# VectorE instead of ScalarE scales the inner rows of a ternary network to integers

## What is computed

```python
def _quant_act(x):
    s = jnp.max(jnp.abs(x), axis=-1, keepdims=True) / 127.0 + EPS
    xq = jnp.clip(jnp.round(x / s), -128.0, 127.0)
    return (xq, s)

def _qlinear(x, w):
    wq, ws = _quant_weight(w)
    xq, xs = _quant_act(x)
    y = jnp.einsum('bsi,oi->bso', xq, wq)
    return y * xs * ws
...
gate = jax.nn.silu(_qlinear(x, w_gate))
up = _qlinear(x, w_up)
return _qlinear(gate * up, w_down)
```

## Time and profile before

| | |
|---|---|
| median of three runs | 478.23 us (477.91 to 479.02) |
| span of the profiled execution, first to last instruction | 476.0 us |
| TensorE busy | 399.1 us |
| VectorE busy | 375.6 us |
| ScalarE busy | 301.7 us |
| granted TensorE clock, mean over the span | 0.956 of full |

### The profile page before, as it was taken

One profiled execution on the slowest core, in us unless ns is written; L12 is line 12 of the kernel. 1 busy time (PEld: TensorE's weight loads), 2 busy tenths in 40 slices (PEclk: granted clock), 3 DMA queues, 4 the chain that ended last, 5 costly groups with the idle time before them and its releaser, 6 DMA issues.

```text
span 476.0 us, 7786 instructions
## 1 busy us (share of the span) xinstructions
PE 399.1 (84%) x2612; PEld 191.0 (40%) x2612; DVE 375.6 (79%) x801; ACT 301.7 (63%) x442; POOL 0.2 (0%) x4
## 2 busy tenths in 40 slices
PE   1041866677786999999999999999999999999996
PEld 1010344333334445544434333554444444444443
DVE  5999599999998989999986975895456677777754
ACT  5888686689795865678976677463234444444422
POOL 0000000000000000000000000000000000000000
PEclk9995699689898899999999999999999999999999
DMA  8520000000003360383433233244413556653101
GB/s 294 227 67 0 1 1 1 1 1 0 2 2 101 121 211 24 93 232 117 138 104 109 89 110 109 83 143 149 145 67 134 170 168 170 169 172 130 67 22 44
DMA packets 31506, 47.47 MB, mean 100 GB/s; under 512 B 5610, under 2 KB 15210, under 8 KB 30956
## 3 DMA queue, kind: packets, MB, share of 16 engines
q1 hardware_dynamic: 31468, 46.98, 31.6%
HBM read 45.65 MB, written 1.31 MB: 99 GB/s over the span
## 4 chain that ended last, share of the span: by engine, by line
PE 60%; DVE 21%; ACT 9%; issue 5%; DMA 2%; SPq 2%; DVEq 0%; ACTq 0%
PE ps L1622 32%; PE ps L1956 16%; PE ps L1731 4%; PE ps L1719 2%; DVE bn L1044 1%; ACT regO L608 1%; SPq L563 1%; DVE xn L1063 1%; PE ps L1741 1%; DMA regC<-in_ctxT_dram 1%; PE ps L1647 1%; ACT regW L629 1%; PE ps L1613 1%; DVE regO L1272 1%; DVE kc L1178 1%
## 5 line engine op out<-in xcount | busy, mean ns | idle before, releaser
L1529 DVE TENSOR_TENSOR regW<-ps,regW 128x512 f32<-128x512 f32 x64 | 44.1, 690 | 53.8 <-PE ps L1622 51.2
L1622 PE MATMUL ps<-hH,regC 128*128 128x512 f16 x264 | 85.5, 379 | 0.0
L959 ACT ACTIVATE regW<-ps 128x512 f32<-128x512 f32 x51 | 30.4, 596 | 85.0 <-PE ps L1622 82.0
L1622 PE MATMUL ps<-hH,regW 128*128 128x512 f16 x248 | 81.5, 384 | 1.1 <-DVE regW L1529 1.1
L1622 PE MATMUL ps<-hL,regC 128*128 128x512 f16 x132 | 50.0, 379 | 0.0
L1956 PE MATMUL ps<-regW,regC 128*128 128x512 f16 x198 | 48.2, 379 | 0.0
L1622 PE MATMUL ps<-hL,regW 128*128 128x512 f16 x124 | 47.5, 383 | 0.0
L1512 DVE TENSOR_TENSOR regW<-regW 128x512 f16<-128x512 f32 x64 | 43.6, 682 | 0.7 <-ACT regW L972 0.5
L1956 PE MATMUL ps<-regW 128*128 128x512 f16 x180 | 43.8, 379 | 0.2 <-DVE regW L1512 0.2
L972 ACT CAST regW<-regW 128x512 f16<-128x512 f32 x64 | 39.2, 613 | 2.0 <-DVE regW L1550 1.8
L1622 PEld LDWEIGHTS ps<-hH,regC 128*128 128x128 f16 x264 | 25.8, 98 | 31.6 <-issue 2.3
(11 more groups left out here) (210 smaller groups left out, 692.2 us busy)
## 6 DMA issues: line engine op xcount, KB each, us to landing
regW<-routing_dram SPq DMA_DIRECT2D x130, 128.0 KB, 3.0
fw<-in_gu_dram SPq DMA_DIRECT2D x31, 256.0 KB, 3.1
regP<-in_gu_dram SPq DMA_DIRECT2D x25, 256.0 KB, 3.1
fw<-in_dp_dram SPq DMA_DIRECT2D x31, 128.0 KB, 3.1
regP<-in_dp_dram SPq DMA_DIRECT2D x25, 128.0 KB, 3.1
regO<-in_ffn_dram SPq DMA_DIRECT2D x3, 1024.0 KB, 9.2
x<-in_x_dram SPq DMA_DIRECT2D x2, 512.0 KB, 8.2
regC<-in_ctxT_dram SPq DMA_DIRECT2D x1, 1024.0 KB, 5.2
```

Source lines behind the costliest of these rows:

```text
L959: nc.scalar.activation(sgm[:, c % 2, :], bank(gate_bank(c)), ACT.Silu, scale=UNSCALE).then_inc(esilu_done, 1)
L1529: V.tensor_tensor(rows, bank(gate_bank(c) + 1), rows, ALU.mult).then_inc(et_done, 1)
L1622: mm = T.matmul(out_ap, w(k), a(k), start=(n == 0), stop=(n == 3 * DK - 1))
```

## The change

VectorE scales each tile at the end of `hidden_scale`, in one instruction (multiply by `rhs`, add MAGIC) that waits for its own reciprocal and, from tile 1 on, for `hz_turned`. ScalarE's `ffn_scale` and its eight calls are gone. What is computed is the same, and no buffer changes.

```diff
@@ BESIDE_SCALAR
             (0, "A"): [("turned_weights", 0, 1), ("weights_high", 5), ("wide_silu", 5, 0, 6), ("weights_high", 6),
-                ("ffn_scale", 4), ("wide_silu", 5, 1, 4)],
+                ("wide_silu", 5, 1, 4)],
             (1, "A"): [("ffn_turned", 4, 6)],
-            (2, "A"): [("ffn_scale", 5), ("wide_silu", 6, 0, 4)],
+            (2, "A"): [("wide_silu", 6, 0, 4)],
...
-            (5, "A"): [("ffn_scale", 7), ("project", 5, 6)],
+            (5, "A"): [("project", 5, 6)],
@@ block.scalar
-            def ffn_scale(t):
-
-                act.wait_ge(hscale_ready, t + 1)
-                if t >= 1:
-                    act.wait_ge(hz_turned, t)
-                nc.scalar.activation(fz, fhp[:, t % 2, :], ACT.Identity, bias=magic[:, 0:1],
-                                     scale=rhs[:, t:t + 1]).then_inc(hz_ready, 1)
...
             ffn_silu(2, 2)
-            ffn_scale(0)
             ffn_silu(3, 4)
             table_exp_ln()
-            ffn_scale(1)
             ffn_turned(0, 4)
-            ffn_scale(2)
             ffn_turned(1, 0)
             ffn_turned(2, 6)
-            ffn_scale(3)
@@ block.vector
                 post(V.tensor_tensor(so[:, t:t + 1], tiny[:, 1:2], wdt[:, :], ALU.mult))
+                dve.wait_ge(hscale_ready, t + 1)
+                if t >= 1:
+                    dve.wait_ge(hz_turned, t)
+                V.tensor_scalar(fz, fhp[:, t % 2, :], rhs[:, t:t + 1], MAGIC, ALU.mult, ALU.add).then_inc(hz_ready, 1)
                 settle()
```

More of the change, by code:

```diff
@@ L343, in bass_flamingo @@
             (0, "A"): [("turned_weights", 0, 1), ("weights_high", 5), ("wide_silu", 5, 0, 6), ("weights_high", 6),
-                ("ffn_scale", 4), ("wide_silu", 5, 1, 4)],
+                ("wide_silu", 5, 1, 4)],
             (1, "A"): [("ffn_turned", 4, 6)],
-            (2, "A"): [("ffn_scale", 5), ("wide_silu", 6, 0, 4)],
+            (2, "A"): [("wide_silu", 6, 0, 4)],
             (2, "B"): [("weights_high", 7)],
             (3, "B"): [("ffn_turned", 5, 4), ("wide_silu", 6, 1, 6), ("weights_high", 8), ("wide_silu", 7, 0, 4),
-                ("ffn_scale", 6), ("weights_high", 9)],
+                ("weights_high", 9)],
             (4, "B"): [("wide_silu", 7, 1, 4), ("ffn_turned", 6, 6), ("high_halves", 8, 6)],
-            (5, "A"): [("ffn_scale", 7), ("project", 5, 6)],
+            (5, "A"): [("project", 5, 6)],
             (5, "B"): [("project", 6, 4), ("ffn_turned", 7, 6), ("weights_high", 10)],
@@ L910, in beside @@
                         exp_logits(*at)
-                    elif name == "ffn_scale":
-                        ffn_scale(*at)
                     elif name == "ffn_turned":
```

## The result

The changed kernel takes 483.28 us (median of 4 runs, 482.50 to 483.59), the kernel before, in the runs beside it, 478.07 (4 runs, 477.54 to 479.02). The ratio is 1.0109 [1.0095, 1.0122], that is 5.2 us slower (4.5 to 5.8). The profiled execution of the changed kernel took 483.59 us, its span 481.8, 5.8 over the span in the earlier trace rows.

What follows compares the result with a forecast made beforehand. VectorE was taken as full in both stretches, with ScalarE's path level in the first. 3.1 plus 1.6 us on the 476.0 span gave 480.7; adding 2.2 for the median gave 482.9, rounded to 483.0, range 481.0 to 486.0.

Steps and rivals of the forecast that it cites:

- the 2.2 us added for the median: Whole kernel: the median of the runs before, 478.23 us, lies 2.2 us over the profiled span of 476.0.
- VectorE full in the first stretch: Tiles 0 to 3, 54 to 71 us: VectorE's only idle stretch before 68 us is 0.30 us; late work stays late.
- The price, 0.75 us, 0.67 net: Each new VectorE scale takes 0.75 us, less 0.08 overlap: 0.67 us net, bounds 0.40 and 1.20.
- Tiles 0 to 3, forecast 3.1: 54 to 71 us: four scales 2.68, plus 0.70 stall at tile 1, less 0.30 gap: 3.1 us, bounds 1.3 and 5.5.
- the forecast 70.5 to 71: First stretch, tiles 0 to 3: the residual that stood at 67.62 us would come at 70.5 to 71.
- Tiles 4 to 7, forecast 1.6: 162 to 190 us: tiles 4 and 5 covered by gaps, 0.25 for hand-offs, tiles 6 and 7 cost 1.34: 1.6 us.
- `low_halves` at 193.5 to 194: End of the second stretch: VectorE's result that TensorE waits for, at 189.11 us before, would come at 193.5 to 194.
- ScalarE's relief at nothing: Both stretches: the eight scales of 1240 ns taken off ScalarE, 9.9 us, give nothing back beyond the replay.
- Not slower: Rival, first stretch: ScalarE's hand-off was the path, so 1.9 us gained, 476.3 us; chance 0.06.
- Only the first stretch: Rival: gaps or a shorter hand-off of tile 6 swallow the second stretch's sum, 481.5 us; chance 0.12.
- one element a cycle: Rival: the new instruction runs at the 1284 ns pace, 0.53 more at six uncovered places, 486.1 us; chance 0.05.
- TensorE's clock falls as well: Rival: TensorE's gap ahead of turning the normed rows grows from 1.25 to 3.0 us, adding 2.0: 485.0 us; chance 0.25.

Runs made afterwards that it cites:

- e6: Kernel before, ScalarE's scales kept, with VectorE also running the same scale instruction into a buffer nobody reads: 481.99 us, ratio 1.0087.
- e5: Kernel before, but ScalarE scales only 8 of 1024 columns of each tile and VectorE gets nothing: 478.68 us, ratio 1.0023.
- e8: Kernel before, with one 128x1024 copy of the attention's preparation moved from VectorE to ScalarE: 477.16 us, ratio 0.9986.
- e4: Against the kernel before, VectorE scales only tiles 6 and 7, ScalarE the rest: 479.37 us, ratio 1.0031.
- e2: Against the kernel before, VectorE scales only tiles 4 to 7, ScalarE tiles 0 to 3: 480.17 us, ratio 1.0040.
- e3: Changed kernel with a second buffer for scaled rows, so a scale waits for the turn of the tile two before: 482.44 us, ratio 1.0098.
- e1: Against the kernel before, VectorE scales only tiles 0 to 3, ScalarE the rest: 481.17 us, ratio 1.0065.
- e7: Changed kernel, but VectorE scales only 8 of 1024 columns of each tile, waits and order kept: 479.15 us, ratio 1.0024.

## Why the prediction was right

Forecast 483.0 us, measured 483.28. The mechanism holds; that the sum meets the time to 0.3 us is in part luck. In the profiles the first stretch is 0.14 us under its forecast, the second 0.61 over (0.73 + 0.25 + 1.23 for 1.6), and the 2.2 us added for the median come from one execution: the changed kernel's median is 1.5 over its profiled span. Step by step:

**VectorE full in the first stretch: shown.** Adding the work to VectorE alone costs +3.8 us (e6). Taking it from ScalarE alone gives 0.26 us in the stretch and no gain in the time (e5). The chain of waits named ScalarE there, and the gap of 0.30 us that the timeline had the earlier trace rows was the whole worth of that name. Apart from it, what VectorE lacks of 12 us from 60 to 72 us is gaps of 0.03 to 0.04 us, as the one from tile 2's product to the reduction that waits for it (62.08 to 62.12), and one of 0.11.

**The price, 0.75 us, 0.67 net.** Measured 753 ns, and 0.67 from its start to that of the next product. Its net cost is 0.61: `so` to the product behind it was 0.18 us and is 0.79 (57.04 to 57.83).

**Tiles 0 to 3, forecast 3.1.** Four times 0.61, plus 0.79 of stall in place of 0.70, less 0.30, is 2.93. The trace shows 2.96, the first half by itself +3.0 in time. The second residual came at 70.02 in the chain, 15.82 behind the product of tile 0 where it was 12.85; the forecast 70.5 to 71 missed it, as the whole stretch started 0.57 earlier.

**Tiles 4 to 7, forecast 1.6.** Tiles 6 and 7: twice 0.61 is 1.22, and the trace shows 1.23; 1.34 was forecast. Two covers were mis-sized. Tile 5's scale was to fall into the gap of 1.70, with 0.25 left for hand-offs. Between tiles 5 and 6 the pair of profiles shows just 0.25, but by luck: in the kernel before, a weight transfer that ScalarE waited 1.24 for the earlier trace rows held that stretch at 9.52. With this wait at 0.58 (e8) and 0.68 (e4), and no new instruction, it is 9.16; with the instruction it is 9.77 in all four kernels that have it (changed, e2, e3, e6). VectorE's gap is 1.53 or 1.54 in all six. The silu that ends it stands on ScalarE behind a cast of VectorE's own routing product (the product starts at 178.59 in the changed kernel, the cast at 179.37, the silu at 180.90). So the gap moves with VectorE and covers nothing, and tile 5 costs its 0.61 unless the transfer is late.

Tile 4's scale did vanish into the wait for the routing row, but idle time of 0.81 stood ahead of the routing product, where the prediction had none. SP began to issue the row's loads 0.42 behind `so` in both profiles (162.63, 166.46), so the scale did not send them late. The product that needs the row came 4.68 us behind `so`, and 4.44 with the second half alone. With the same instruction at tile 4 it came at 3.97 (e3) and 3.96 (e6), without idle, and without the instruction between 3.90 (e4) and 4.34 (e5). So the transfer's spread among kernels without the instruction covers 0.39 of the 0.73 that came too late; whether the rest is spread as well or the change's is open. By time the second half costs 2.0 [1.1, 2.7], which 1.6 lies within.

**`low_halves` at 193.5 to 194: it came at 195.15,** for the attention's 1.42 us and the routing row's 0.73, less the 0.57 of the earlier start.

**ScalarE's relief at nothing: shown** for the first stretch by e5 and e6, and by e5 for the time as a whole.

**The rivals.** *Not slower* is refuted by e5 and e6. What the shorter instruction saves (0.49 us each, eight times) did not show in the time, as the work went to VectorE, which was busy 10.96 of 12 us in the first stretch. *Only the first stretch* is refuted by e2 and e4, *one element a cycle*, the pace of the 1284 ns row, by the 753 ns.

*TensorE's clock falls as well* came true in part, and with it one of the signs that the prediction named for being wrong: the granted clock was 0.50 at 75 us. The gap ahead of the turn of the normed rows is 2.08 us and not 3.0, since tile 3's turn itself waited 1.10 for the residual and started at 70.56. This gap is 2.08 or 2.09 in the six kernels in which an engine does other work for tiles 0 to 3 than before (changed, e1, e3, e5, e6, e7), and 1.25 or 1.26 in the four others (before, e2, e4, e8). In the 6 us behind it the granted clock is 0.72, 0.75, 0.61, 0.72, 0.50 and 1.00 in the six, and 1.00 in each of the four.

At that place it cost the changed kernel nothing: from the statistics to VectorE's copies of the turned keys both profiles take 13.4 us (68.14 to 81.52, 70.53 to 83.92), as VectorE is the bound there and not TensorE: it is busy 12.47 us in both, TensorE 9.50 and 10.07, at a granted clock of 1.00 and 0.87. In the profiles of e6 and e3 the same stretch takes 13.66 and 14.08. In the changed kernel's profile what can be the clock's cost came later, between the scans that start at 90.63 and 101.74 before (11.11 us) and at 93.03 and 105.47 after (12.44), at a granted clock of 0.66 where it was 0.92: 1.33 us. The second half alone has 12.38 there, with no change ahead of it, so one profile does not put this part down to the change.

The executions taken together do show a difference. A mean granted clock of 0.940 or less stands in 9 of the 44 executions of the six kernels (1 of 4, 2 of 6, 2 of 5, 4 of 12, none of 5 and none of 12), and in none of the 90 of the four, whose lowest is 0.942. In e1, e3 and e5 these executions take 1.8, 1.4 and 2.7 us more than the others, by the medians, near the 2.0 that the rival was priced at; the changed kernel's single one (483.07) does not. So the lower clock is more frequent with the wider gap. That the gap is its cause is likely and not shown, since no run moves the gap by itself. The rival's 2.0 us was the author's estimate, and no run shows it; what they show in its place is those three differences, and in the traces the turning of eight blocks, 2.07 us at a granted clock of 0.50 and 1.04 at 1.00. In the medians little room is left for its cost: 3.0 us against 3.17 in the first half's own stretch, 2.0 against 0.50 + 0.25 + 1.21 in the second's, 5.2 [4.5, 5.8] against 2.96 + 0.73 + 0.25 + 1.23 for the whole.

## What to carry to other kernels

Before work moves from one engine to another, look at the idle time of the engine that receives it, in the very stretch, and not at the name that the chain of waits gives: two paths can run level, and a cheaper instruction (0.75 in place of 1.24 us) on the full one cost 5.2 us here. Replay the order by hand, the wait that comes along included: one such wait was 0.79 of 2.96 us. Relief need not be free: with ScalarE's scale nearly gone and VectorE not charged (e5), TensorE idled 2.08 in place of 1.25 us, and four of 12 executions had a lower mean clock than any before. And do not explain a difference between two profiles by the change until a kernel without that part of it has been seen in the same place.

## What was not expected of the hardware

TensorE's mean granted clock varies between executions of one and the same code. Of the kernel with tiles 0 to 3 alone, six executions took 479.95 us at a mean granted clock of 0.957 up to 482.82 at 0.938. In the stretch from 94 to 100 us, where kernel and order are those of before, the granted clock was 1.00 before, 0.58 with tiles 4 to 7 alone and 0.72 with tiles 6 and 7 alone, and the time between the two scans 11.11, 12.38 and 12.41 us.

An instruction of 8 columns still took 0.23 us on VectorE (e7) and 0.39 on ScalarE (e5), against 0.75 and 1.24 for 1024: near a third of either price stays with under a hundredth of the columns.
